# A 3x3 convolution in fp32 on four 64x64 tiles, from a padded image that the normalisation writes

## What is computed

```python
    x = x + _L0_conv_ref(_ln_c(x), ...)                  # first layer: a block of 1x1 products
    t = _to_tokens(x)
    t = t + _L0_ffn_ref(_ln_t(t), ...)                   # first mixture, 2 of 8 experts per image, ends in a layer norm
    x = _from_tokens(t, x)
    x = x + _L1_conv_ref(_ln_c(x), L1_conv_w)            # 3x3, 64 -> 64 channels, padding 1, divided by 9
    t = _to_tokens(x)
    t = t + _L1_ffn_ref(_ln_t(t), ...)                   # second mixture, 2 of 8 experts per token
```

## Time and profile before

| what | us |
|---|---|
| median of 3 runs | 318.09 |
| lowest and highest of them | 316.52, 319.81 |
| profiled execution, span from first to last instruction | 315.9 |
| TensorE busy in it | 285.4 |
| VectorE busy | 173.6 |
| ScalarE busy | 169.8 |
| mean granted clock, share of the full one | 0.972 |

### The profile page before, as it was taken

How to read it: one execution, slowest core, us unless ns; L and a number is a source line. 1 busy time by engine, 2 the same in 40 slices (tenths; PEclk the granted TensorE clock), 3 DMA queues, 4 the chain that set the end, 5 groups by cost and what they waited for, 6 DMA issues and landing times.

```text
span 315.9 us, 6360 instructions
## 1 busy us (share of the span) xinstructions
PE 285.4 (90%) x2342; PEld 146.5 (46%) x2342; DVE 173.6 (55%) x404; ACT 169.8 (54%) x328; POOL 35.6 (11%) x74
## 2 busy tenths in 40 slices
PE   6999999895678998797999999999999999999993
PEld 4555253264544444784976534533333333333441
DVE  3677967675521367868984174673333334443433
ACT  3722235225364754535423566466677777777772
POOL 8126445200152000000000000000000000000000
PEclk9999999999568999999979999999999999999999
DMA  7648788660000000000000896000069920800010
GB/s 203 227 93 186 186 188 180 143 240 2 0 0 1 2 0 3 0 0 2 1 2 9 200 211 124 2 0 2 1 124 225 203 60 3 168 0 2 9 29 17
DMA packets 11566, 24.09 MB, mean 76 GB/s; under 512 B 2192, under 2 KB 4400, under 8 KB 11408
## 3 DMA queue, kind: packets, MB, share of 16 engines
q1 hardware_dynamic: 9808, 19.19, 25.8%
q0 software_dynamic: 1328, 3.84, 5.8%
q10 hardware_dynamic: 400, 0.66, 0.8%
HBM read 14.73 MB, written 1.33 MB: 51 GB/s over the span
## 4 chain that ended last, share of the span: by engine, by line
PE 62%; DVE 11%; ACT 8%; SPq 8%; issue 5%; DMA 4%; ACTq 1%; DVEq 1%; POOL 0%
PE PS L777 19%; PE PS L755 18%; SPq L395 8%; PE PS L709 7%; PE PS L497 3%; DMA moved<-amp 3%; PE PS L663 3%; PE PS L519 2%; PE PS L681 2%; PE PS L536 2%; DMA X<-x_in 2%; DVE D L1278 2%; ACT amp L926 1%; ACT h L926 1%; ACT Q L813 1%
## 5 line engine op out<-in xcount | busy, mean ns | idle before, releaser
L755 PE MATMUL PS<-N,late 64*64 64x512 f32 (+1 forms) x640 | 77.7, 549 | 0.0
L926 ACT ACTIVATE amp<-PS,late 128x512 f32<-128x512 f32 (+1 forms) x80 | 47.2, 640 | 22.4 <-PE PS L755 22.0
L926 ACT ACTIVATE h<-PS,late 128x512 f32<-128x512 f32 (+1 forms) x80 | 47.2, 641 | 18.1 <-PE PS L755 17.6
L755 PEld LDWEIGHTS PS<-N,late 64*64 64x64 f32 x640 | 26.5, 133 | 33.7 <-issue 32.0
L777 PE MATMUL PS<-h,late 64*64 64x512 f32 (+1 forms) x320 | 39.5, 556 | 1.5 <-DVE D L1278 0.9
L777 PE MATMUL PS<-amp,late 64*64 64x512 f32 (+1 forms) x320 | 39.2, 552 | 0.7 <-ACT amp L926 0.3
L1278 DVE SCALAR_TENSOR_TENSOR D<-PS,late,moved 128x512 f32<-128x512 f32 (+1 forms) x24 | 14.8, 658 | 33.6 <-PE PS L777 31.5
L1278 DVE SCALAR_TENSOR_TENSOR D<-PS,late,img 128x512 f32<-128x512 f32 x16 | 11.3, 746 | 34.9 <-PE PS L777 34.9
L1284 DVE TENSOR_TENSOR X<-D,X 128x512 f32<-128x512 f32 (+1 forms) x40 | 25.4, 634 | 2.1
L709 PE MATMUL PS<-img,conv_hl 128*128 128x288 f32 x144 | 23.3, 321 | 0.7 <-DVE amp L1208 0.4
L709 PEld LDWEIGHTS PS<-img,conv_hl 128*128 128x128 f32 x144 | 21.9, 203 | 3.0 <-issue 2.9
(11 more groups left out here) (151 smaller groups left out, 322.8 us busy)
## 6 DMA issues: line engine op xcount, KB each, us to landing
img<-gates_hbm SPq DMA_DIRECT2D x4, 1024.0 KB, 14.5
moved<-amp SPq DMA_DIRECT2D x40, 96.0 KB, 3.9
moved<-amp POOLq DMA_DIRECT2D x35, 96.0 KB, 3.4
moved<-gates_hbm SPq DMA_DIRECT2D x4, 512.0 KB, 8.1
moved<-gates_hbm SPq DMA_DIRECT2D x2, 1024.0 KB, 10.6
late<-late_in SPq DMA_DIRECT2D x1, 1852.0 KB, 7.7
moved<-gates_hbm SPq DMA_DIRECT2D x4, 256.0 KB, 5.8
mix<-mix_in SPq DMA_DIRECT2D x1, 897.0 KB, 10.0
```

What stands on the lines that cost most here:

```text
L755: mm = pe.matmul(PS[64 * r:64 * r + 64, 2 * (n % RING) + half, 0:w], L("w1")[rows, u:u + 64], N[rows, a:a + w], start=True, stop=True, ski ...
L926: act.activation(hid(n, half)[:, 0:w], PS[:, 2 * (n % RING) + half, 0:w], ACT.Gelu, bias=L("b1")[:, BLOCKS * g + b:BLOCKS * g + b + 1]).th ...
```

## The change

The split into a high and a low part goes. VectorE's product of norm 3 is written straight into `img`, now four padded images on 128 partitions (`PAIRS` instead of `BATCH`) in plain fp32, in pieces that end where an image ends. `split_conv`, `parts` and ScalarE's `conv` are gone, and so is the buffer `clow`.

`conv p` is now a whole pair. For each tap it issues four fp32 matmuls on the four 64x64 tiles: half `h` of the partitions, part `j` of the image's rows, to output partitions `64 * (h ^ j)` of bank `j`. VectorE reads the result: scaled and added to `X` in one operation, one for `j = 0` on 128 partitions, two on 64 for `j = 1`, since there the halves come out swapped. `gB` for odd spans has a buffer of its own. In the cut diff below, the first `conv` is TensorE's; the branch for `i == 3` is in VectorE's `spread`; the last `conv` is VectorE's.

```diff
-CONV_PAIR = [1, 2, 1, 2, 3, 3, 3, 3]
+CONV_PAIR = [1, 2, 3, 3]
-        img = sb("img", [128, BATCH, PADN], F32R)
+        img = sb("img", [128, PAIRS, PADN])
+        gB_odd = sb("gB_odd", [128, EXP * 512])
...
-            def conv(n):
...
+            def conv(p):
+                pe.wait_ge(late_ld, 16)
+                pe.wait_ge(LN[3]["normed"], chunks_for(p))
...
+                for tap in range(TAPS):
+                    dy, dx = tap // 3, tap % 3
+                    for half in range(2):
+                        q = slice(64 * half, 64 * half + 64)
+                        for j in range(2):
+                            o = 64 * (half ^ j)
+                            mm = pe.matmul(PS[o:o + 64, 2 * CONV_PAIR[p] + j, 0:HALFPIX], w[q, tap, :],
+                                           iv[q, j * ROWS + dy:j * ROWS + dy + ROWS, dx:dx + WD],
+                                           start=tap == 0, stop=tap == TAPS - 1, skip_group_check=True)
...
+                elif i == 3:
+                    for p, y0, ny in pieces(c):
+                        a, n = p * PIX + y0 * WD, ny * WD
+                        iv = img[:, p, :].rearrange("p (y z) -> p y z", z=PADW)
+                        last = ve.tensor_tensor(iv[:, 1 + y0:1 + y0 + ny, 1:1 + WD],
+                                                PS[:, ln_bank(3, c), a - c * BANK:a - c * BANK + n].rearrange("p (y z) -> p y z", z=WD),
+                                                D[:, a:a + n].rearrange("p (y z) -> p y z", z=WD), ALU.mult)
...
+            def conv(p):
+                ve.wait_ge(conv_mm, p + 1)
+                for j in range(2):
+                    a = p * PIX + j * HALFPIX
+                    for lo, hi in ([(0, 128)], [(0, 64), (64, 128)])[j]:
+                        o = 64 * j - lo if j else 0
+                        last = ve.scalar_tensor_tensor(out=X[lo:hi, a:a + HALFPIX], in0=PS[o:o + hi - lo, 2 * CONV_PAIR[p] + j, 0:HALFPIX],
+                                                       scalar=1.0 / TAPS, in1=X[lo:hi, a:a + HALFPIX], op0=ALU.mult, op1=ALU.add)
+                last.then_inc(x3_done, 1)
...
-        center 2 3, down0 3 1, spread 3 0, spread 3 1, spread 3 2, center 2 4, center 2 5, root 2 1, conv 0, conv 1, spread 2 3, conv 2, conv 3, center 4 0,
+        center 2 3, down0 3 1, spread 3 0, spread 3 1, spread 3 2, center 2 4, center 2 5, conv 0, root 2 1, conv 1,
```

## The result

The changed kernel is **slower**, by 1.4%: 321.92 us (321.58 to 324.0, four runs) where before took 317.53 beside it, a ratio of 1.0136, interval 1.0095 to 1.0177, clear of no change but short of 2%. The profiled execution has a span of 320.4 us. The forecast was 313.9, at most 318.5, and faster.

The account below looks back on a forecast made before the run. It took TensorE, busy for 90% of a 315.9 us span, as the bound. Span: 315.9 - 5.9 gain + 1.7 clock fall = 311.7; runs: 318.1 - 4.2 = 313.9 us, range 311 to 318.5.

Parts of the forecast that it names:

- The convolution: TensorE's convolution: 18 rounds of 0.242 plus 0.1, 4.5 us per pair, 17.9 for four, 4.5 less than before.
- The rival of the shared reader: Convolution: two streams of one 64-row half share a reader, a round is 0.29, 3.2 us more; chance 0.25.
- that of the banks: Convolution: two row halves writing one bank take turns, 17.5 us more, 331.4, slower; chance 0.10.
- Read-outs: VectorE's three operations after each pair's convolution: 0.5 us each, 1.5 per pair, bounds 0.4 and 0.6.
- The stations up to the first mixture step: TensorE's start times: first convolution 126.5, `center 4 0` 136.3, logits 148.2, first mixture steps 151.9 for 162.39 before.
- The clock: TensorE near the logits: one fall to 0.50 as long as before, 3.4, on streaming work, costing 1.7 us.
- the 5.9 at the full clock: Gain by `root 4 1`: 5.0 from reaching it at 180.0 for 185.02, plus one more step done, 0.86.
- After that TensorE has mixture steps for every wait: Behind `root 4 1`: the gain there, counted in mixture steps done, is the gain in all; 0 lost to the end.
- Up to `down0 3 1` nothing that counts differs: Stretch ahead of where the two layers meet: same time as before, a difference of 0.
- The waits: TensorE stands between logits and turns: 1.7 for a gate operation, 1.3 at pair 2, 1.9 at the turns.
- the 174 that the text names as a sign of being wrong: First gate load from HBM: expected about 172.5, wanted by VectorE about 174.2; landing after 174 would show the forecast wrong.
- The gain is eaten by the order: Rival: a longer wait, or a second clock fall around the turns, another 1.7, 315.6; chance 0.08.

Follow-up runs that it names:

- b2: Changed kernel with fillers around the first logits, one step less ahead of the first late spread, and VectorE's gate copies ahead of its pair 2 read-out; 0.9851 of before.
- a1: Changed kernel with seven fillers between the first logits and first mixture step, three ahead of the third pair's convolution; 316.57 us, 0.9941 of before.
- d1: New convolution in the order of the kernel before, without the 17 fillers from `spread 4 0` to pair 2's convolution; 0.9943 of before, 0.9858 with them.
- d2: Kernel before, with the old convolution, without 17 fillers between `spread 4 0` and the convolution of pair 2; 320.13 us, 1.0049 of before.
- a3: Changed kernel with one more mixture step between `root 4 1` and its first spread, the total of steps unchanged; 1.0108 of before.
- a5: Changed kernel with one mixture step less between `root 4 1` and its first spread, and one more at the end; 0.9958 of before.
- a4: Changed kernel with the second router logits in three parts, a mixture step between them, instead of one piece; 1.0113 of before.
- a2: Changed kernel with the first logits in bank 5, so that the first two mixture steps need no gate operation; 0.9974 of before.

## Why the prediction was wrong, step by step

- **The convolution: right.** 72 records in 4.53 us from start to next start where 4.5 was said, and 4.37 behind the mixture, whose tile shape it shares (173.68 to 178.04): a round of 0.2425. The rival of the shared reader (0.29; its price by these figures is 72 x 0.048, 3.5 rather than 3.2) and that of the banks (0.485) are out. The rule of the Trainium skill, TensorEngine Tiling (Array Packing), section Gotcha 1: PSUM Pressure, that different row tiles cannot access one bank at once, does not show here: two row halves write one bank, in different partitions, at full rate.
- **Read-outs: right,** 1.39 for three where 1.5 was said.
- **The stations up to the first mixture step: right.** Less the 1.18 by which the execution was late at the first spread: first convolution 126.5 (said 126.5), `center 4 0` 136.3 (136.3), logits 148.4 (148.2), first step 152.0 (151.9), with the gap of 1.52 that a gate operation ends (said 1.7).
- **The clock: the step that failed.** "I take one fall of the same length, on mixture steps or on pair 2, work that streams throughout: half of 3.4, 1.7 us." That it falls near the logits was right, its length was not: 13.65. Pair 2 ended at 166.1 (less 1.18) for 160.8, the turns at 169.0 for 163.6, and `root 4 1` is 5.5 late, 185.5 for 180.0. Beyond the 1.7 it is 3.8. In the kernel before a convolution without a break followed the fall; in the changed one a stand of 1.52, two steps, and spreads with waits. The text said that there was "less work than in the stretch after which it fell before", and still took that stretch's length. The rest of the sum to `root 4 1` held: b2, whose clock did not fall there, is 6.4 ahead of before at equal steps, 1.1 of it by the early gate copies, so 5.4 for the 5.9 at the full clock. That the new order with its few fillers made the low clock longer is shown by a1, d1 and d2 together; why it was 13.65 and not 3.4 or 6.8 is open.
- **"After that TensorE has mixture steps for every wait": failed.** 3.73 us were lost there. The extra step done by `root 4 1`, counted as a gain, moved every later piece by one place, from ahead of a team's first down step to behind it: 1.7 for the waits, 0.3 for a gate operation on ScalarE, and 1.7 for a fall behind the second logits.
- **"Up to `down0 3 1` nothing that counts differs": right of the program,** not of the execution: +1.18, inside the spread of 122.1 to 127.0 that twelve profiles of this same stretch have.
- **The waits: right in sum,** 4.3 between logits and turns for 4.9. The first gate load landed at 176.6, behind the 174 that the text names as a sign of being wrong, but cost nothing: VectorE's first use, at 180.97, waited for TensorE. "The gain is eaten by the order", a second fall around the turns, was the nearest rival and far too small: 1.7, where the two steps that failed lost 7.5.

The three misses, 3.8 + 3.7 + 1.2, are the 8.7 between 311.7 and 320.4.

## What to carry to other kernels

Price a shorter stretch on TensorE with the clock it leaves behind: when a change takes fillers or other work from beside waits and narrow matmuls, the low clock can last several times as long as it did, and a run with fillers in the stands shows about what it costs. Steps done early are a gain only if the pieces behind them still stand where they covered a wait, so check the place of every later piece, not the count. When an improvement comes together with a new order, time it in the old order too.

## What the runs showed of the hardware

- Plain fp32 matmuls on four 64x64 tiles keep 0.2425 us a round at 288 columns, reading rows of 24 out of 26 and with two row halves writing one bank; neither costs anything at that pace.
- The low clock's length is not a constant of an order: a3 and a5 had 13.65 us behind the first logits as the changed kernel, a4, with the same order there, twice 3.4 (mean granted clock 0.961 or 0.962 in all four of its executions). a1 fell behind the second logits, a2, with the same order there, did not. What decides it is open.
- Up to the first spread of the third normalisation twelve of these profiles run one and the same program, and took 122.1 to 127.0 us; the kernel before (with and without the fillers further on) took 123.4 and 126.2, with the clock at 0.50 for 13.7 us there in the one and 23.9 in the other. This scatter, up to 4.9 us or 1.5% of the span, lies in every comparison of single profiles here, which is why the stations are compared from the first spread on.
